# A two-layer graph and attention network in float32: 125-row transfers in two pieces, row statistics in another stage, and an edge layer on halves of the rows

## The reference

```python
x = x + scatter_add(dst, (LN(x) @ W)[src] * edge_weight) + bias     # layer 0, graph
f = LN(x)                                                            # layer 0, ffn
u = f + attention(LN(f) * g1 + b1) @ wo
x = x + u + experts_top2(LN(u) * g2 + b2)                            # 64 experts
n = LN(x)                                                            # layer 1, graph
s0, s1 = n[:, :128] @ Wu0, n[:, 128:] @ Wu1                          # node rows
h = edge_feats                                                       # [20000, 8]
for W in (W_mlp1, W_mlp2, W_mlp3):                                   # the edge network
  h = silu_gain * silu(h @ W / sqrt(W.shape[0]))                     # 64 wide
x = x + segment_sum(products of h @ W_mlp4, s0[src], s1[src], edge_attrs) @ Wout / 10
f = LN(x)                                                            # layer 1, ffn
route = softmax(gelu(mean_over_nodes(f) @ router_w1.T + b) @ router_w2.T + b)
spatial, temporal = argmax(route[:4]), argmax(route[4:])             # two experts
fused = cross_attention(spatial_attention(LN(f) * ws + bs), temporal_attention(LN(f) * wt + bt))
u = f + fused
x = x + u + gelu(LN(u) * wm + bm @ mlp_w1.T) @ mlp_w2.T              # 2048 hidden
```

## Time and profile before

| | |
|---|---|
| runs | 3545.56 us median of 3 (3540.73 to 3550.62) |
| profiled execution | 3546.62 us |
| its span (first to last instruction) | 3544.6 us |
| mean granted TensorE clock | 0.917 of full speed |
| PE busy | 2874.9 us, 81% |
| PEld busy | 2020.3 us, 57% |
| DVE busy | 1924.2 us, 54% |
| ACT busy | 1455.4 us, 41% |
| POOL busy | 1117.0 us, 32% |
| moved by DMA | 413.07 MB, mean 117 GB/s |

### The profile page before, as it was taken

How to read it: one execution, slowest core, us unless ns; L and a number is a source line. 1 busy time by engine, 2 the same in 40 slices (tenths; PEclk the granted TensorE clock), 3 DMA queues, 4 the chain that set the end, 5 groups by cost and what they waited for, 6 DMA issues and landing times. The chain is left out here.

```text
span 3544.6 us, 46725 instructions
## 1 busy us (share of the span) xinstructions
PE 2874.9 (81%) x15443; PEld 2020.3 (57%) x15443; DVE 1924.2 (54%) x3884; ACT 1455.4 (41%) x3150; POOL 1117.0 (32%) x1141
## 2 busy tenths in 40 slices
PE   0404876999947995869999698978999889997898
PEld 0201225777645663534444685558777687775776
DVE  6203773477633113569998425652677536775533
ACT  0100003466502542546666425542566435663322
POOL 4777764367103443066665000000000000001210
PEclk9857997999967997989999799999999999999999
DMA  3104765533136995354443265213422044311322
GB/s 101 40 6 126 210 184 173 134 58 64 38 107 201 343 340 158 134 182 140 145 137 90 87 196 112 55 50 123 132 55 65 8 149 108 84 36 37 98 76 77
DMA packets 231423, 413.07 MB, mean 117 GB/s; under 512 B 48860, under 2 KB 146442, under 8 KB 227092
## 3 DMA queue, kind: packets, MB, share of 16 engines
q1 hardware_dynamic: 174532, 273.61, 26.4%
q0 software_dynamic: 56208, 136.40, 14.2%
q10 hardware_dynamic: 448, 0.08, 0.0%
HBM read 318.32 MB, written 95.47 MB: 117 GB/s over the span
## 5 line engine op out<-in xcount | busy, mean ns | idle before, releaser
L875 ACT ACTIVATE at_p<-at_pb,at_max 125x1250 f32<-125x1250 f32 (+4 forms) x320 | 383.5, 1198 | 302.3 <-DVE at_unused L946 273.1
L762 PE MATMUL at_pb<-ident,at_p 125*125 125x125 f32 x2880 | 433.9, 281 | 20.5 <-ACT at_p L875 17.4
L762 PEld LDWEIGHTS at_pb<-ident,at_p 125*125 125x125 f32 x2880 | 391.0, 191 | 82.9 <-ACT at_p L875 23.7
L779 PE MATMUL at_pb<-at_pt,at_v 125*64 125x250 f32 x2880 | 355.8, 384 | 5.2 <-DVE s_t L979 3.0
L1407 PE MATMUL so_ps<-g_got,g_hot 128*125 128x512 f32 x332 | 179.2, 634 | 201.7 <-DMA g_got<-support,g_edges 169.9
L939 DVE TENSOR_REDUCE at_wide<-at_pb 125x1 f32<-125x1024 f32 x240 | 293.5, 1223 | 21.4 <-PE at_pb L745 2.8
L722 PE MATMUL at_pb<-at_s,at_shared 128*128 128x500 f32 (+1 forms) x1152 | 230.2, 362 | 63.6 <-DVE at_shared L898 53.9
L861 ACT ACTIVATE at_pt<-at_pb 125x500 f32<-125x500 f32 (+1 forms) x448 | 232.3, 519 | 95.4 <-PE at_pb L762 91.4
L686 POOL TENSOR_TENSOR s_t<-s_t,at_all 128x500 f32<-128x500 f32 (+1 forms) x36 | 45.0, 1250 | 671.5 <-DVE s_t L979 651.1
L722 PEld LDWEIGHTS at_pb<-at_s,at_shared 128*128 128x128 f32 x1152 | 197.0, 195 | 96.4 <-issue 54.3
L779 PEld LDWEIGHTS at_pb<-at_pt,at_v 125*64 125x64 f32 x2880 | 188.6, 137 | 103.9 <-issue 14.5
(11 more groups left out here) (305 smaller groups left out, 5542.1 us busy)
## 6 DMA issues: line engine op xcount, KB each, us to landing
w_ring<-in_L_ffn_w SPq DMA_DIRECT2D x128, 512.0 KB, 11.0
at_shared<-k_parts SPq DMA_DIRECT2D x64, 312.5 KB
ml_w<-in_mlp_w SPq DMA_DIRECT2D x64, 256.0 KB
k_parts<-at_shared SPq DMA_DIRECT2D x64, 250.0 KB, 3.1
q_parts<-at_shared SPq DMA_DIRECT2D x64, 250.0 KB, 2.9
h_edges<-em_both SPq DMA_DIRECT2D x11, 1024.0 KB, 4.3
g_h<-h_edges SPq DMA_DIRECT2D x11, 1024.0 KB, 5.5
at_shared<-q_parts SPq DMA_DIRECT2D x32, 312.5 KB
```

Of the source, the lines that this page charges most:

```text
L762: ins = pe.transpose(pturn[0:TN, g % 2, TN * (t % 4):TN * (t % 4) + TN], p[:, u % 2, TN * t:TN * t + TN], c.ident[0:TN, 0:TN])
L779: ins = pe.matmul(pout[side:side + 64, 0:2 * TN], v[:, t, 2 * j + h, :], p_t[:, q % 2, t, :], start=(t < 2), stop=(t >= keys[u] - 2))
L875: act.activation(p[:, t % 2, 0:w], score[t % 2][0:TN, 0:w], ACT.Exp, bias=neg_max[:, t:t + 1], accum_out=total[:, t:t + 1]).then_inc(exp_d ...
```

## The change

- **Transfers in two.** Stores and loads on 125 partitions are made as two: rows 0 to 111 (`MOST = 112`) and rows 112 to 124 (13 rows). This holds for x, z, `support`, `nodes`, the residual, `x1` and `x4` as parts, the five edge arrays of each placement, and the output. Semaphore counts rise with them (32 where it was 16).
- **Kept rates.** `normalize` with `double` no longer computes or stores y: `ln_y`, `xa` and `xc` are gone. The first rate and shift of each row stay in SBUF (`keep0` for layer 0, another for layer 1, `[125, 2, 10]`). `out_tokens` loads the unnormalized rows `x1` or `x4` in place of `xa` or `xc`, and ACT, after its high parts, applies rate and shift to each tile (ten activations, semaphore `normed`). POOL's bias additions and, without a bias, DVE's residual additions wait for `normed` in place of the loads.
- **Row statistics.** `bn_stats` of tile i follows the addition that completes the tile: in `out_tokens`, and in the last pass of `graph_sum1`. They go to `c.stats`, kept in SBUF, and the normalize stages behind (the second, the router's, the last) are called with `counted=True` and skip them.
- **The router's mean.** It is taken from x: DVE makes `weight`, each row's first rate times 1/1250, and TensorE multiplies this column by the tile's 512 columns of x, one such matmul after each of the first ten groups of transposes, into one bank of one row. DVE copies that row (`mean`), and TensorE turns it into a column with four one-column matmuls; four more, on `spread` (the sum of the row's shifts, in all columns) and the column of 1/1250, add the shifts.
- **The edge network's third layer.** `w3` is `[128, 128]`, without zeros. A half's two matmuls contract over 64 rows each: rows 0 to 63 and rows 64 to 127, into two banks. `three(g-3, 0)` stands ahead of `two(g-2)`, `three(g-3, 1)` where `three(g-3)` was; ACT follows in the same order, and DVE takes the quarters as they come. One `memset` fewer.

The core of the diff (indentation halved):

```diff
+MOST = 112
+def in_two(dst, src):
+  return (dst[0:MOST], src[0:MOST]), (dst[MOST:TN], src[MOST:TN])
...
-def normalize(nc, c, x, x_out=None, first_out=None, last_out=None, double=False, targets=(), router=None):
...
+    stats = c.stats if counted else sb("ln_stats", [TN, NT, 6])
...
+    root, second = (sb(f"ln_{n}", [TN, NT]) for n in ("root", "second"))
+    first, shift = (keep[:, 0, :], keep[:, 1, :]) if double else (sb("ln_first", [TN, NT])[:, :], None)
...
+          for to, of in in_two(tiles_of(x_out), x[:, :, :]):
+            sp.dma_start(to, of).then_inc(stored, 16)
+          n += 32
...
-        if first_out is not None:
-          sp.wait_ge(y_made, NT)
-          sp.dma_start(tiles_of(first_out), y[:, :, :]).then_inc(stored, 16)
-          n += 16
+          for to, of in in_two(tiles_of(last_out), z[:, :, :]):
+            sp.dma_start(to, of).then_inc(stored, 16)
+          n += 32
...
         if router:
...
-        for i in range(NT):
-          own.mark(dve.bn_stats(stats[:, i, :], x[:, i, :]))
-        own.join()
+        if not counted:
+          for i in range(NT):
+            own.mark(dve.bn_stats(stats[:, i, :], x[:, i, :]))
+          own.join()
...
+        if router:
+          own.mark(dve.tensor_reduce(shifts[:, :], shift, AX, ALU.add))
+          dve.tensor_scalar(weight[:, :], first, c.mean_col[0:TN, :], None, ALU.mult).then_inc(weighed, 1)
+          own.join()
+          own.mark(dve.tensor_scalar(spread[:, :], c.iota[0:TN, 0:128], 0.0, shifts[:, :], ALU.mult, ALU.add))
         for i in range(NT):
           dve.tensor_scalar(z[:, i, :], x[:, i, :], mv[:, i, 0:1], rate[:, i:i + 1], ALU.subtract, ALU.mult)\
             .then_inc(normed, 1)
...
         if router:
+          own.join()
           dve.wait_ge(pool_sum, 1)
-          dve.tensor_copy(pooled[:, :], ps[:, BANKS, 0:DC]).then_inc(pool_ready, 1)
+          dve.tensor_copy(mean[:, :], ps[0:1, BANKS, :]).then_inc(mean_out, 1)
+          dve.wait_ge(pool_turned, 1)
+          dve.tensor_copy(pooled[:, :], ps[:, BANKS + 1, 8:8 + DC]).then_inc(pool_ready, 1)
...
-        if double:
-          act.wait_ge(scaled, 1)
-          for i in range(NT):
-            act.activation(y[:, i, :], x[:, i, :], ACT.Identity, bias=shift[:, i:i + 1], scale=first[:, i:i + 1])\
-              .then_inc(y_made, 1)
...
           ins.then_inc(turned, 1)
+          if router and n < NT:
+            if n == 0:
+              pe.wait_ge(weighed, 1)
+            ins = pe.matmul(ps[0:1, BANKS, :], weight[:, n:n + 1], x[:, n, :], start=(n == 0), stop=(n == NT - 1))
+            if n == NT - 1:
+              ins.then_inc(pool_sum, 1)
         if router:
-          for i in range(NT):
-            pe.wait_ge(y_made, i + 1)
-            for k in range(DC):
-              ins = pe.matmul(ps[:, BANKS, k:k + 1], y[:, i, 128 * k:128 * k + 128], c.mean_col[0:TN, :],
-                      start=False, stop=(i == NT - 1 and k == DC - 1))
-          ins.then_inc(pool_sum, 1)
+          pe.wait_ge(mean_out, 1)
+          for k in range(DC):
+            pe.matmul(ps[:, BANKS + 1, 8 + k:9 + k], mean[:, 128 * k:128 * k + 128], c.ident[0:1, 0:1],
+                 start=True, stop=False)
+            ins = pe.matmul(ps[:, BANKS + 1, 8 + k:9 + k], spread[:, :], c.mean_col[0:TN, :], start=False, stop=True)
+          ins.then_inc(pool_turned, 1)
           pe.wait_ge(pool_ready, 1)
...
+              for to, of in in_two(tiles_of(out_d)[:, i, :], res[:, i, :]):
+                sp.dma_start(to, of).then_inc(stored, 16)
...
-        sp.dma_start(res[:, 0:4, :], tiles_of(residual_d)[:, 0:4, :]).then_inc(res_in, 16)
+        for to, of in in_two(res[:, 0:4, :], tiles_of(before_d)[:, 0:4, :]):
+          sp.dma_start(to, of).then_inc(res_in, 16)
...
-            pool.wait_ge(res_in if i < 4 else res_in2, 16)
+            pool.wait_ge(normed, i + 1)
       @block.scalar
       def _(act):
         high(act)
+        for i in range(NT):
+          act.wait_ge(res_in if i < 4 else res_in2, 32)
+          act.activation(res[:, i, :], res[:, i, :], ACT.Identity, bias=keep[:, 1, i:i + 1], scale=keep[:, 0, i:i + 1])\
+            .then_inc(normed, 1)
...
-            dve.wait_ge(res_in if i < 4 else res_in2, 16)
+            dve.wait_ge(normed, i + 1)
           dve.tensor_tensor(y[:, i, :], ps[0:TN, i % 8, :], res[:, i, :], ALU.add).then_inc(added, 1)
-        dve.wait_ge(added, NT)
+          dve.wait_ge(added, i + 1)
+          dve.bn_stats(c.stats[:, i, :], y[:, i, :]).then_inc(counted, 1)
+        dve.wait_ge(counted, NT)
...
+        for to, of in in_two(key[:, :], key_d.rearrange("(p t) -> p t", p=TN)):
+          sp.dma_start(to, of).then_inc(loaded, 16)
...
-        def three(t):
-          for q in range(4):
-            n, half = q // 2, q % 2
-            pe.wait_ge(a2, 2 * t + half + 1)
-            if 4 * t + q >= 2:
-              pe.wait_ge(a3, 4 * t + q - 1)
-            pe.matmul(ps[:, 4 + q % 2, :], w3[:, n, :], h[:, 1, t % 2, half * HW:(half + 1) * HW],
+        def three(t, half):
+          pe.wait_ge(a2, 2 * t + half + 1)
+          if 2 * t + half >= 1:
+            pe.wait_ge(a3, 4 * t + 2 * half)
+          for n in range(2):
+            r = slice(64 * n, 64 * n + 64)
+            pe.matmul(ps[:, 4 + n, :], w3[r, :], h[r, 1, t % 2, half * HW:(half + 1) * HW],
                  start=True, stop=True).then_inc(s3, 1)
...
             up_nodes(nodes[0])
+          if 0 <= g - 3 < GROUPS:
+            three(g - 3, 0)
           if 0 <= g - 2 < GROUPS:
             two(g - 2)
           if nodes:
             turn_nodes(nodes[1])
           if 0 <= g - 3 < GROUPS:
-            three(g - 3)
+            three(g - 3, 1)
           if nodes:
             up_nodes(nodes[1])
...
               dve.wait_ge(st[t % 2], 16 * (t // 2))
+            for m in range(4):
+              half, n = m // 2, m % 2
+              q = 2 * n + half
+              dve.wait_ge(a3, 4 * t + m + 1)
...
           if g == AGGR:
...
-        act.wait_ge(zeroed, 3)
+        def third(t, half):
+          if t < 0:
+            return
+          for n in range(2):
+            m = 4 * t + 2 * half + n
+            act.wait_ge(s3, m + 1)
+            if m >= 2:
+              act.wait_ge(low, m - 1)
+            act.activation(h3[:, n, :], ps[:, 4 + n, :], ACT.Silu, scale=SILU_GAIN / 8).then_inc(a3, 1)
...
-            act.dma_start(w3[64 * n:64 * n + 64, n, 64 * m:64 * m + 64], w_d[2]).then_inc(wts, 16)
+            act.dma_start(w3[64 * n:64 * n + 64, 64 * m:64 * m + 64], w_d[2]).then_inc(wts, 16)
...
             keep_nodes(nodes[0])
+          third(g - 3, 0)
           layer(1, g - 2)
...
+          third(g - 3, 1)
           if nodes:
             keep_nodes(nodes[1])
...
+          dve.wait_ge(left, i + 1)
+          dve.wait_ge(added, i + 1)
+          dve.bn_stats(c.stats[:, i, :], x[:, i, :]).then_inc(counted, 1)
+        dve.wait_ge(counted, NT)
...
-        normalize(nc, c, x_sb, x_out=x1, first_out=xa, double=True, targets=[(s_t, col("ln1_g"), col("ln1_b"))])
+        keep0 = s0("keep0", [TN, 2, NT])
+        normalize(nc, c, x_sb, x_out=x1, keep=keep0, targets=[(s_t, col("ln1_g"), col("ln1_b"))])
-        out_tokens(nc, c, s_t, wo, late[0], xa)
+        out_tokens(nc, c, s_t, wo, late[0], x1, keep0)
-      normalize(nc, c, x_sb, last_out=z2, targets=[(s_t, col("ln2_g"), col("ln2_b"))])
+      normalize(nc, c, x_sb, last_out=z2, counted=True, targets=[(s_t, col("ln2_g"), col("ln2_b"))])
```

More of the change, by code:

```diff
@@ L280, in _ @@
             def _(pe):
-                if router:
-                    pe.wait_ge(nil_made, 1)
-                    pe.matmul(ps[:, BANKS, 0:DC], nil[:, :], nil[:, 0:DC], start=True, stop=False)
                 for n, (g, k) in enumerate(turns):
```

133 lines of the change are left out of this document (63 added, 70 removed).

## The result

The changed kernel takes 3459.66 us, the median of four runs (3454.87 to 3463.48), the kernel before 3543.38 with a fourth run beside it; the ratio is 0.976, 95% interval 0.974 to 0.978. The forecast was 3462.5. The profiled execution has a span of 3458.2 us, 86.4 less than before; the forecast sum was 83.2.

What follows compares the result with a forecast made beforehand. No single engine bounds the whole; stages end at barriers, where 125-row transfers at a third of the rate hold them when last. Terms sum to 83.2 us off 3546.6, giving 3463.4, stated as median 3462.5; range 3447 to 3481.

Steps and rivals of the forecast that it cites:

- The first layer norm: First layer norm stage: with `xa` no longer stored, the next stage starts at about 544.1 instead of 566.64, -22.5 us.
- the router's: Router's layer norm: without `ln_y` and 40 one-column matmuls, pooled copy 27.3 us after stage start instead of 38.3; sum -10.3.
- the last: Last layer norm: statistics leave the path, -6.0 and +0.7, together -5.3 us.
- the end's wait: Kernel end: the last four output stores, for which SP waits 7.1 us, finish sooner when split, -5 us.
- the rate applications: Both output stages: ScalarE's ten, 0.80 us each, hidden by TensorE's 120 matmuls; otherwise up to 8 us each time.
- Rival 1: Splitting doesn't widen: 112 rows go at 128 GB/s, `xa` gives 20, total 3502 us; chance 6%.
- The z store: Second layer norm: split store takes 8.0 us instead of 21.3, -13.3; with statistics moved, the term is -18.6.
- the rule against this edit: Second layer norm's split store: two transfers to two partition ranges serialize, 6% measured; the sum would be the first rival's.
- Placing: Edge placements: faster split loads, less five more issues, -5.5 us in the first; -2 in the second.
- The MLP: MLP's change of groups: split stores no longer delay the next weights, where TensorE idled 7.89 us; -9 us.
- The edge network: Edge network's third layer: pairs save 0.6 us in five groups, 3; new order 2; sum -5, bounds +1 and -12.
- At nothing: Support, nodes and residual stores and loads elsewhere: no gain, as POOL, TensorE or VectorE is later.

Runs made afterwards that it cites:

- experiment 8: Changed kernel with row statistics taken in the three normalize stages again, none behind the additions: 3533.27 us on its chip, ratio 0.9819.
- experiment 1: Changed kernel with every 125-row transfer whole again, kept rates, moved statistics and edge layer left as changed: 3498.49 us, ratio 0.9866.
- experiment 7: Changed kernel with the store of zeros held back in the first placement until the edge arrays have landed: placing 38.41 us, VectorE starting at 12.42.
- the second profile: Changed kernel unaltered, profiled again on another chip: 3546.05 us, ratio 0.9772 to the kernel before.
- experiment 2: Kernel before with only the routing stage's load of part x1 split into 112 and 13 rows: 3544.41 us, routing 65.54, experts 271.44.
- experiment 6: Changed kernel with POOL's ten additions of the part held back until VectorE has shifted the logits: routing 70.05 us, experts 269.57.
- experiment 10: Kernel before with 240 and 80 unused bytes per partition set aside in SBUF: experts 269.52 us, total 3634.11 on its chip.

## Why the prediction was right, and where it was not

**Right by its steps.** The first layer norm gave 23.0 for 22.5, the router's 10.2 for 10.3, the last 4.9 for 5.3, the end's wait fell by 4.8 for 5. The output stages hide the rate applications (VectorE's additions there wait for TensorE alone), and experiment 8 confirms the price of the statistics. Rival 1, splitting doesn't widen, is what experiment 1 builds: forecast at 3502, measured at 3498.49, and the first layer norm without splitting gave 20.5 for the 20 stated there.

**The z store** missed by 1.5 us. The step that failed: "For the 112-row piece I take 400 GB/s, the row nearest to it". The piece uses all engines, as said, but each moves 20.4 GB/s and not 25, and the 13-row piece adds a tail. As for the rule against this edit, from the Trainium skill, "SBUF — State Buffer", section "Can I just issue two DMAs to hit both halves?" (two transfers to two partition ranges serialize): the trace agrees in that the seven full microseconds move just the 2.29 MB of the large piece and the small one finishes behind it, yet the wait falls from 21.3 to 9.8, since the large one alone has 16 engines and the whole had 5.

**Placing** missed by 3.4. The step: "1.2 MB at 128 GB/s are 9.4 us. At 400 they are 3.0". The issues cost more than allowed: the last of the ten ends at 8.58 and the last of the five at 6.29, 2.3 us and not at most 1.8. The forecast also left out the 1.36 MB of zeros, which now share the engines with the wide loads (experiment 7: 0.8 and 1.5 us, about the scatter of other profiles). The rest is open.

**The MLP** missed by some 2 (by 1 in the second profile, whose stall is 0.7). The step: "Afterwards twelve issues of 0.34 end near 3441.4 instead of 3442.6, and 1.5 MB at 400 GB/s are gone by then". An issue takes 0.44 with the gap behind it, so twelve took as long as six had, and the transfers moved 260 GB/s at that time; the weights landed 5.2 us behind their issue, and 1.89 us of stall were left.

**The edge network** was forecast at 5 and is worth 6.1 when the chance in its start is set aside (3.9 and 7.3 with it), but not by the terms of the sum. The step that failed: "A lone pair would by this take 3 steps and not 4", with a gain of 0.6 in five groups, and 2 for the order beside it. A pair takes 1.13 and not 1.41 us. Nor do the two add: the pairs alone lose 0.2 a period (10.92), the order alone gives 0.17 (10.56), both together 1.1, or 5.5 in the five groups where 3 were forecast. The Trainium skill, "TensorEngine Tiling (Array Packing)", section "Theoretical Speedup", has up to 2x for this contraction; the pair itself reached 1.66.

**At nothing** stood the routing stage, with "POOL, TensorE or VectorE is later". Its step is wrong: the load of the part decides when POOL adds, and so which VectorE operations it slows (experiments 2 and 6). The experts' 3.8 us could be seen as a wait of TensorE for weights, 3.2 us in the kernel before (experiment 2), but not that the edit would end it: two buffers of 320 bytes in all do that (experiment 10).

So the mechanisms of the large terms were right, and that the total came within 3 us of its forecast is in part luck: 8.2 us of shortfall met 6.4 from stages put at nothing and 4.8 from stages that the change doesn't touch.

## What to carry to other kernels

A row count of transfers is worth choosing by its divisors: 112 and 13 rows for 125 took more than half off the wait for a store that was last, and with 113 and 12 the stage took 81 us longer than with those. Where two engines and two PSUM banks pass work around, a faster instruction and a better order may each give nothing and both together a tenth of the period, so such edits are tried together before either is dropped. A stage that waits for nothing can still change when a load lands earlier, because an engine is then busy beside other instructions.

## What was not expected of the hardware

- The place of buffers in SBUF changes how fast full-width transfers run: with 320 bytes more set aside ahead of them, 351 GB/s for 337 at the same share of the engines, and issues of 508 ns for 1056.
- 120 rows (with 5 beside them) use 15 engines and are slower than 112 on 16 by far more than that: 203 GB/s against 327.
- VectorE's comparison of 125x640 elements takes 1.83 us beside POOL's additions and 0.82 without, and POOL's additions take up to 1.73 for 1.26.
- Three chips ran the kernel before in 3547, 3601 and 3627 us, and nearly all of the difference lies in two stages: 46.2 and 40.6 of the 87.5 us between the profile of the kernel before and that of experiment 10, in the first layer's stage and the first attention.
